# Order of index copies and exponentials on ScalarE in the first graph aggregation of a two-layer GNN and mixture-of-experts kernel

## The chip, the cores and the metric

The kernel runs on one core of one Trainium2 chip. The metric is the device time of one execution in microseconds, the median of several runs. The profile is of one execution on the same core.

## The reference

Four layers act on x, 3125 nodes by 256 features: an attention aggregation over a graph of 53125 edges, a mixture of eight experts, a weighted aggregation over the same graph with a batch norm, and a graph-routed mixture of four experts. The change lies in the first, which is, cut to what is computed:

```python
h = x @ Wn.T + bn                       # x layer-normed, 3125 x 256
e = edge_attr @ We.T + be
a = leaky_relu(sum((h[src] + e) * attn, axis=-1), 0.01)
m = segment_max(a, dst, num_segments=N)
a = exp(a - m[dst])
denom = segment_sum(a, dst, num_segments=N)
a = a / (denom[dst] + 1e-16)
out = relu(segment_sum(h[src] * a[..., None], dst, num_segments=N))
x = x + out
```

## The kernel before, in words

The edges are sorted by destination. They lie in chunks of 128 edges, one edge to a partition, and the destinations in 25 tiles of 128 nodes (`NT`). `emit_aggregate` (called twice, the first time with `softmax` true and the tag `a0`, the second time with the tag `a1`) sums, for every destination tile, over blocks of `BG` = 6 chunks. Most tiles have three blocks, some four, and there are 77 blocks, so 462 chunks with those that lie across a tile's edge counted twice. For the chunk at place `i` of block `g`:

- ScalarE copies the column of 128 source numbers into `idx[:, i]` (L574) and counts `indexed`.
- GpSimd (POOL) waits for that count and issues an indirect DMA, which gathers 128 rows of `h`, with a one behind each, from the table in HBM into `rows[:, i]` (L589).
- VectorE (DVE) writes for a whole block at once a mask `nb`: minus the tile's maximum where edge and destination belong together, and minus 1e30 besides where they don't (L722 and L726), into a ring of `RING` = 4 blocks. It counts `masked`.
- ScalarE makes the weights `w[:, i]` as the exponential of mask plus score (L789) and counts `weighed`.
- TensorE (PE) waits for the gather and for the weights and adds `w` transposed times `rows` to the tile's sum in PSUM (L619, two passes for float32), then counts `agg_done`, which frees `rows`, `idx` and `w` at place `i` alike.

The tiles' maxima are made ahead. During tile t VectorE masks the blocks of t (`mask_blocks`), adds the finished sum of t - 1 to x (`finish_tile`, L734 to L740) and then scans tile t + 2 (`scan`): for each of its blocks six masks (L684) and six maxima (L701), then one reduction (L704). PE transposes the result (L602, `find_max`), VectorE reduces it (L708, `negate_max`) and PE spreads it over the partitions (L606, `spread_max`); `keep_max` copies it into `negm` (L716), which is the first thing that VectorE does in a tile. PE's own order in tile t is: `find_max(t + 1)`, opening the sum (L612), the first block, `spread_max(t + 1)`, the other blocks, closing the sum (L623).

ScalarE's order is written out by hand. In every block there were six copies, each with its own wait for the freed place, then one wait for the mask, then six exponentials:

```python
put_indices(act, g, c)
act.wait_ge(masked, g + 1)
for i in range(BG):
    act.wait_ge(agg_done, g * BG + i + 1)
    nc.scalar.activation(w[:, i, :], ...)
```

where `put_indices` is

```python
for i in range(BG):
    act.wait_ge(agg_done, g * BG + i + 1)
    nc.scalar.copy(idx[:, i:i + 1], source[:, bass.ds(c + i, 1)]).then_inc(indexed, 1)
```

The blocks are a hardware loop (L783) in a loop over tiles (L780), whose bounds each engine loads from SBUF at a tile's start (L488).

Of the kernel before, what the change touches and what calls it, by code (L numbers as in the profile page):

```python
# [502 lines left out]
def emit_aggregate(nc, S, tag, table, softmax):  # L503
# [6 lines left out]
    indexed, agg_done, masked, weighed = sem(tag + "_idx"), sem(tag + "_agg"), sem(tag + "_msk"), sem(tag + "_w")  # L510
    best, best_t, negs, negs_w, closed, evac = (sem(f"{tag}_{n}") for n in ("best", "bestT", "negs", "negsW", "closed", "evac"))
    width = D + 1 if softmax else D
    with ExitStack() as ctx:
        sb = lambda n, s, d: ctx.enter_context(nc.sbuf_tensor(tag + n, s, d))
        idx = sb("idx", [P, BG], I32)
# [17 lines left out]
        source = S.src if softmax else S.esource  # L533
# [37 lines left out]
        def put_indices(act, g, c):  # L571
# [4 lines that stand above are left out]
        @block.gpsimd  # L576
        def _(pool):
            if softmax:
                total = tile_range(nc, pool, S, NT - 1)[0]
            else:  # L580
                total = pool.value_load(S.eranges[0:1, NT:NT + 1], min_val=1, max_val=EBLOCKS)
            count = pool.alloc_register(tag + "_count")
            pool.reg_mov(count, 0)
            with pool.Fori(0, total) as g:
                for i in range(BG):
                    pool.reg_add(count, count, 1)
                    pool.wait_ge(indexed, 1)
                    pool.wait_ge(indexed, count)
                    pool.indirect_dma_start(rows[:, i, 0:TW], None, table,  # L589
                                            bass.IndirectOffsetOnAxis(ap=idx[:, i:i + 1], axis=0)).then_inc(gathered[i], 16)  # L590
# [184 lines left out]
        @block.scalar  # L775
        def _(act):
            nc.scalar.preload_act_table(ACT.Exp)
            act.sem_inc(weighed, (RING - 1) * BG + 1)
            tiles = Tiles(act, "act")
            with act.Fori(0, NT) as t:  # L780
                tiles.load(t)
                tiles.step()
                with tiles.blocks() as g:  # L783
                    c = tiles.chunk(g)
                    put_indices(act, g, c)
                    act.wait_ge(masked, g + 1)
                    for i in range(BG):
                        act.wait_ge(agg_done, g * BG + i + 1)
                        nc.scalar.activation(w[:, i, :], nb[:, bass.ds(g % RING, 1), i, :].rearrange("p a n -> p (a n)"), ACT.Exp, bias=S.score[:, bass.ds(c + i, 1)]).then_inc(weighed, 1)  # L789


# [1049 lines left out]
```

## Time and profile before

| | us |
|---|---|
| median of 3 runs (lowest, highest) | 3857.48 (3857.24, 3864.25) |
| the profiled execution | 3854.0 |
| its span, first to last instruction | 3851.9 |
| first aggregation in it | 704 to 1515 |
| busy in the whole span: PE, DVE, ACT, POOL | 2660.5, 1510.2, 759.3, 1889.8 |

A time of the profile counts from the first instruction. An engine's idle time before an instruction is given with what ended it; "issue" means that nothing which the profile shows was waited for. PEld is TensorE's weight load, DVEq and ACTq are the instructions that a sequencer works off itself (registers, branches, waits); the page does not count these as busy.

### The profile page before, as it was taken

How to read it: one execution, taken by the hardware profiler on the slowest of the kernel's cores; microseconds unless marked ns; L12 is line 12 of the kernel's file. 1: busy time of each engine (PE TensorE's matmuls, PEld its weight loads, DVE VectorE, ACT ScalarE, POOL GpSimd, SP SyncE). 2: the span in 40 equal slices, each digit the busy share in tenths (PEclk: the TensorE clock that was granted, in tenths of full speed). 3: DMA queues.
4: the chain of work that ended last, by engine and by line, in shares of the span. 5: the costliest groups of instructions: out<-in, count | busy, mean ns of one | idle time of the engine just before them, and what ended most of it. 6: DMA issues, size and time to landing. Idle time of an engine off the chain costs nothing. (4 is left out here: it accounts for less than half of the span.)

```text
span 3851.9 us, 46754 instructions
## 1 busy us (share of the span) xinstructions
PE 2660.5 (69%) x10550; PEld 1816.4 (47%) x10551; DVE 1510.2 (39%) x3666; ACT 759.3 (20%) x2605; POOL 1889.8 (49%) x1926
## 2 busy tenths in 40 slices
PE   3249688465566556699999997677777755989900
PEld 2225587233333333576767665333333334666600
DVE  5774555656666653322222223322222233000075
ACT  0136000123322222222222221111111112222200
POOL 0000666265656554366666663366666611666602
PEclk9555555566666665799999998666666665999955
DMA  2012344132222222100000000233333311110001
GB/s 73 27 38 66 143 146 147 33 83 75 79 79 79 74 76 61 33 11 12 12 12 12 14 1 20 77 91 91 91 89 92 89 26 34 20 20 8 9 36 36
DMA packets 124782, 213.24 MB, mean 55 GB/s; under 512 B 56098, under 2 KB 82807, under 8 KB 122423
## 3 DMA queue, kind: packets, MB, share of 16 engines
q0 software_dynamic: 75808, 125.28, 13.1%
q1 hardware_dynamic: 48918, 87.37, 6.7%
q8 instruction: 18, 0.29, 0.0%
q14 instruction: 38, 0.30, 0.0%
HBM read 196.99 MB, written 15.52 MB: 55 GB/s over the span
## 5 line engine op out<-in xcount | busy, mean ns | idle before, releaser
L589 POOL DMA_INDIRECT a0rows<-table,a0idx x462 | 466.3, 1009 | 363.0 <-ACT a0idx L574 250.5
L589 POOL DMA_INDIRECT a1rows<-table,a1idx x444 | 420.1, 946 | 315.3 <-ACT a1idx L574 176.6
L619 PE MATMUL a1ps<-a1rows,a1w 128*128 128x256 f32 x888 | 435.5, 616 | 173.2 <-DMA a1rows<-table,a1idx 115.9
L619 PE MATMUL a0ps<-a0rows,a0w 128*128 128x257 f32 x924 | 428.3, 602 | 153.6 <-ACT a0w L789 71.4
L1053 POOL DMA_INDIRECT erecords<-k_rece x416 | 404.5, 972 | 213.3 <-issue 103.2
L881 PE MATMUL f0up<-k_xnT,f0w 128*128 x1280 | 386.0, 457 | 59.4 <-ACT f0hid L913 33.7
L1053 POOL DMA_INDIRECT records<-k_recg x288 | 301.0, 1045 | 226.1 <-POOLq L959 74.2
L1373 POOL DMA_INDIRECT gt_land<-table_gat,gt_source x281 | 265.9, 946 | 287.7 <-DVEq L1402 141.7
L619 PEld LDWEIGHTS a1ps<-a1rows,a1w 128*128 128x128 f32 x888 | 215.5, 284 | 393.2 <-issue 278.2
L619 PEld LDWEIGHTS a0ps<-a0rows,a0w 128*128 128x128 f32 x924 | 233.5, 286 | 345.8 <-issue 176.6
L891 PE MATMUL f0dn<-f0w,f0hid 128*128 128x256 f32 x1600 | 357.6, 380 | 9.2 <-issue 8.6
L881 PEld LDWEIGHTS f0up<-k_xnT,f0w 128*128 128x128 f32 x1280 | 246.5, 199 | 193.3 <-issue 57.7
L891 PEld LDWEIGHTS f0dn<-f0w,f0hid 128*128 128x128 f32 x1600 | 304.1, 190 | 56.2 <-issue 14.6
L832 DVE SCALAR_TENSOR_TENSOR k_x<-f0dn,k_gate,k_x 128x256 f32 (+1 forms) x200 | 88.9, 479 | 507.5 <-PE f0dn L891 330.1
L913 ACT ACTIVATE f0hid<-f0up,f0b1now 128x384 f32<-128x384 f32 (+1 forms) x320 | 167.7, 528 | 539.8 <-PE f0up L881 327.8
L658 DVE TENSOR_SCALAR a1w<-k_iota,k_elane,k_eweight 128x128 f32<-128x128 f32 x444 | 148.1, 370 | 266.1 <-PE a1ps L619 149.5
L1610 PE MATMUL f1dn<-gt_arena 128*128 128x256 f32 x800 | 191.0, 388 | 28.6 <-issue 24.3
L1600 PE MATMUL f1up<-k_xnT,gt_arena 128*128 x640 | 187.5, 449 | 23.5 <-DVE gt_arena L1417 14.1
L574 ACT COPY a1idx<-k_esource 128x1 int32 x444 | 82.7, 191 | 578.5 <-PE a1ps L619 351.8
L789 ACT ACTIVATE a0w<-a0nb,k_score 128x128 f32 x462 | 143.7, 389 | 235.1 <-DVE a0nb L726 183.0
L471 PEld LDWEIGHTS es_ps<-k_we_attn,es_ea 128*128 128x128 f32 x832 | 182.1, 332 | 5.6 <-issue 5.3
L1610 PEld LDWEIGHTS f1dn<-gt_arena 128*128 128x128 f32 x800 | 152.8, 193 | 62.1 <-issue 42.3
(387 smaller groups left out, 3133.3 us busy)
## 6 DMA issues: line engine op xcount, KB each, us to landing
es_ea<-in_eaT SPq DMA_DIRECT2D x16, 1664.0 KB
es_lane<-lane_row SPq DMA_DIRECT2D x16, 832.0 KB
so_rowl<-glane_row SPq DMA_DIRECT2D x32, 256.0 KB
a0rows<-table,a0idx POOLq DMA_INDIRECT x462
a1rows<-table,a1idx POOLq DMA_INDIRECT x444
erecords<-k_rece POOLq DMA_INDIRECT x416
table<-k_tbl SPq DMA_DIRECT2D x10, 650.0 KB, 3.6
records<-k_recg POOLq DMA_INDIRECT x288
```

Source lines behind the costliest of these rows:

```text
L471: nc.tensor.matmul(ps[i][:, 2, c:c + 1], ea[:, i, c * P:(c + 1) * P], S.we_attn[:, 0:1], start=True, stop=True).then_inc(step, 1)
L589: pool.indirect_dma_start(rows[:, i, 0:TW], None, table, bass.IndirectOffsetOnAxis(ap=idx[:, i:i + 1], axis=0)).then_inc(gathered[i], 16)
L619: nc.tensor.matmul(sum_of(t), w[:, i, :], rows[:, i, 0:width], start=False, stop=False).then_inc(agg_done, 1)
L658: nc.vector.tensor_scalar(w[:, i, :], S.iota[:, 0:P], S.elane[:, bass.ds(c + i, 1)], S.eweight[:, bass.ds(c + i, 1)], ALU.is_equal, ALU.mu ...
L789: nc.scalar.activation(w[:, i, :], nb[:, bass.ds(g % RING, 1), i, :].rearrange("p a n -> p (a n)"), ACT.Exp, bias=S.score[:, bass.ds(c + i ...
L881: ins = nc.tensor.matmul(up[q % 2][:, 0:size], w1[:, k, m * P:(m + 1) * P], S.xnT[:, k, bass.ds(g * (U * P) + a * P, size)], start=(k == 0 ...
L891: ins = nc.tensor.matmul(down[j][:, 0:D], hid[half][:, k, (j - a) * P:(j - a + 1) * P], w2[:, k, :], start=(k == 0), stop=(k == KH - 1))
L913: nc.scalar.activation(hid[half][:, m, :], up[q % 2][:, 0:(b - a) * P], ACT.Gelu, bias=bias_now[:, m:m + 1]).then_inc(hid_ready, 1)
L1053: pool.indirect_dma_start(self.rec_dram, bass.IndirectOffsetOnAxis(ap=self.rec[:, c + 1, 0:1], axis=0), self.rec[:, c + 1, 1:R], None).the ...
L1373: pool.indirect_dma_start(land[:, j, :], None, S.table_gat, bass.IndirectOffsetOnAxis(ap=source[:, j:j + 1], axis=0)).then_inc(gathered[la ...
L1600: ins = nc.tensor.matmul(up[q % 2][:, 0:size], w1[:, k, m * P:(m + 1) * P], S.xnT[:, k, bass.ds(g * (U * P) + a * P, size)], start=(k == 0 ...
L1610: ins = nc.tensor.matmul(down[j][:, 0:D], hid[half][:, k, (j - a) * P:(j - a + 1) * P], w2[:, k, :], start=(k == 0), stop=(k == KH - 1))
```

## The change

ScalarE, in the first aggregation alone, no longer copies six indices ahead of the wait for the block's mask. It waits for the mask first, and then makes for every place `i` one copy and one exponential, behind one wait for the freed place. `put_indices` remains for the second aggregation. The two other engines' programs are as before.

```diff
@@ -782,10 +782,10 @@
                 tiles.step()
                 with tiles.blocks() as g:
                     c = tiles.chunk(g)
-                    put_indices(act, g, c)
                     act.wait_ge(masked, g + 1)
                     for i in range(BG):
                         act.wait_ge(agg_done, g * BG + i + 1)
+                        nc.scalar.copy(idx[:, i:i + 1], source[:, bass.ds(c + i, 1)]).then_inc(indexed, 1)
                         nc.scalar.activation(w[:, i, :], nb[:, bass.ds(g % RING, 1), i, :].rearrange("p a n -> p (a n)"), ACT.Exp, bias=S.score[:, bass.ds(c + i, 1)]).then_inc(weighed, 1)
```

On ScalarE (the engine ACT), inside the loop over blocks, before the change; `a0idx` is `idx`, `k_src` the source numbers, `a0w` the weights and `a0nb` the mask, and an ISA row is a register or wait instruction. Here are the last two copies and the first two exponentials of a block:

```order
L574 ISA
L574 COPY a0idx<-k_src 128x1
L573 REGISTER_ALU
L574 ISA
L574 COPY a0idx<-k_src 128x1
L786 REGISTER_ALU
L789 ISA
L789 ACTIVATE a0w<-a0nb,k_score 128x128
L789 ISA
L789 ACTIVATE a0w<-a0nb,k_score 128x128
```

A block's six copies stand ahead of the wait for its mask (L786) and its exponentials behind it.

The same place after the change, two of a block's six pairs:

```order
L787 REGISTER_ALU
L788 ISA
L788 COPY a0idx<-k_src 128x1
L789 ISA
L789 ACTIVATE a0w<-a0nb,k_score 128x128
L787 REGISTER_ALU
L788 ISA
L788 COPY a0idx<-k_src 128x1
L789 ISA
L789 ACTIVATE a0w<-a0nb,k_score 128x128
```

Every copy now stands behind the wait for the block's mask and right ahead of the exponential of the same place.

## Rows read from the trace of the kernel before

**Rows 1.** Groups by line, 700 to 1515 us (busy us, mean ns, idle before them).

```profile
L619 PE MATMUL a0ps<-a0rows,a0w 128*128 128x257 f32 x924 | 428.3, 602 | 153.6 <-ACT a0w L789 71.4 <-DMA a0rows<-table,a0idx 59.8 <-issue 19.1
L789 ACT ACTIVATE a0w<-a0nb,k_score 128x128 f32 x462 | 143.7, 389 | 235.1 <-DVE a0nb L726 183.0 <-issue 46.0
...
L777 ACT ACT_TABLE_LOAD x1 | 1.3, 1283 | 310.9 <-PEq L306 310.9
```

**Rows 2.** Waits of 700 to 1515 us (total us, times, longest).

```profile
PEld a0psT L602 <- DVE a0top L704: 127.5, 18, 28.4
...
DVE a0rden L734 <- PE a0ps L623: 34.1, 2, 18.8
```

**Rows 3.** Line 716, a tile's first DVE instruction: ns, first and last start.

```profile
L716 DVE COPY a0negm<-a0psM x25: 280/292/293, 732.4 to 1471.6; 128x128 f32<-128x128 f32 x25
```

**Rows 4.** Timeline around the tile from 1108.76 us, part of it.

```profile
1108.76 0.29 DVE L716 COPY a0negm<-a0psM 128x128 f32<-128x128 f32 x1 [0.20 <-issue]
...
1112.04 1.86 ACT L789 ACTIVATE a0w<-a0nb,k_score 128x128 f32 x6 [8.99 <-DVE a0nb L726]
1112.17 0.29 DVE L708 TENSOR_REDUCE a0m<-a0psT 128x1 f32<-128x128 f32 x1 [0.34 <-issue]
...
1114.91 1.46 POOL L589 DMA_INDIRECT a0rows<-table,a0idx  x1 [4.65 <-ACT a0idx L574]
...
1122.37 1.26 DVE L684 TENSOR_SCALAR a0mb<-k_iota,k_dstf 128x128 f32 x6 [0.51 <-issue]
...
1126.41 0.75 DVE L684 TENSOR_SCALAR a0mb<-k_iota,k_dstf 128x128 f32 x2 [0.73 <-issue]
...
1129.65 0.94 POOL L589 DMA_INDIRECT a0rows<-table,a0idx  x1 [0.30 <-issue]
...
1132.53 0.70 PE L619 MATMUL a0ps<-a0rows,a0w 128*128 128x257 f32 x2 [0.42 <-DMA a0rows<-table,a0idx]
...
1133.05 1.08 ACT L574 COPY a0idx<-k_src 128x1 int32 x6 [4.47 <-PE a0ps L619]
...
1134.01 1.01 POOL L589 DMA_INDIRECT a0rows<-table,a0idx  x1 [3.41 <-ACT a0idx L574]
1135.16 1.26 DVE L684 TENSOR_SCALAR a0mb<-k_iota,k_dstf 128x128 f32 x6 [0.70 <-issue]
...
1139.50 0.29 DVE L716 COPY a0negm<-a0psM 128x128 f32<-128x128 f32 x1 [0.20 <-issue]
```

**Rows 5.** Sequencer instructions of line 684 and line 780, 1126 to 1132.5 us.

```profile
L684 DVEq FUSED_REGOPS  x6: 15/700/712, 1127.5 to 1132.4; - x6
...
L780 ACTq COMPARE_BRANCH  x1: 700/700/700, 1130.3 to 1130.3; - x1
```

**Rows 6.** Timeline of the four-block tile from 794.5 us: DVE, ACT, POOL.

```profile
815.32 0.51 DVE L684 TENSOR_SCALAR a0mb<-k_iota,k_dstf 128x128 f32 x2 [0.73 <-issue]
...
827.96 1.27 DVE L684 TENSOR_SCALAR a0mb<-k_iota,k_dstf 128x128 f32 x6 [0.70 <-issue]
...
817.69 0.19 ACT L574 COPY a0idx<-k_src 128x1 int32 x1 [1.94 <-issue]
...
823.58 0.94 POOL L589 DMA_INDIRECT a0rows<-table,a0idx  x1 [1.69 <-ACT a0idx L574]
```

**Rows 7.** DVE's timeline of the tiles from 1327.8 and from 1365.2 us.

```profile
1348.42 0.68 DVE L684 TENSOR_SCALAR a0mb<-k_iota,k_dstf 128x128 f32 x3 [0.73 <-issue]
...
1360.81 1.27 DVE L684 TENSOR_SCALAR a0mb<-k_iota,k_dstf 128x128 f32 x6 [0.98 <-issue]
...
1379.18 0.48 DVE L684 TENSOR_SCALAR a0mb<-k_iota,k_dstf 128x128 f32 x2 [0.95 <-issue]
...
1387.99 1.35 DVE L684 TENSOR_SCALAR a0mb<-k_iota,k_dstf 128x128 f32 x6 [0.73 <-issue]
```

**Rows 8.** Timeline of the last two tiles: first products of the earlier one, last close.

```profile
1461.29 5.36 PE L619 MATMUL a0ps<-a0rows,a0w 128*128 128x257 f32 x12 [0.95 <-ACT a0w L789]
...
1512.05 1.22 PE L623 MATMUL a0ps<-k_iota,k_zeros 1*128 1x257 f32 x2
```

## The prediction

> **What bounds the kernel now.** The change touches the first aggregation alone, 704 to 1515 us, so I read that stretch: first the groups by line, for how busy each engine is and what ended its idle time, then the waits, then the timeline of one tile for the order of events. PE's products take 428.3 of some 811 us and ScalarE's exponentials 143.7 [rows 1]; neither is full. ScalarE's idle time ahead of the exponentials is 235.1 us, of it 183.0 on VectorE's mask [rows 1]. PE waits 127.5 us, 18 times, for VectorE's scan [rows 2]. VectorE on the other side waits for PE at the sums 34.1 us in all, but only twice, with 18.8 the longest, where the work runs out [rows 2]. So **VectorE paces the tiles**: its first instruction of a tile starts 25 times, from 732.4 to 1471.6 us [rows 3], 30.8 us apart on average, and in the tile that I show from 1108.76 to 1139.50, 30.7 us [rows 4].
>
> Within that tile the reader is to see two things. First, ScalarE's exponentials wait 8.99 us for the mask and start at +3.3 us (1112.04), while the six copies for the same block had been made as soon as the places were free; those of the next tile stand at 1133.05, ten microseconds ahead of its mask [rows 4]. Copies, gathers and their latency lie under VectorE's scan. Second, the scan has **a dragging spell**. One block of it, from masks to masks, takes 4.04 us (1122.37 to 1126.41), the next one 8.75 us (1126.41 to 1135.16) [rows 4]. In the spell the register instructions ahead of the masks take 700 ns in the median, and so does ScalarE's branch at the tile's end [rows 5]. The spell begins at 1127.5 [rows 5], 12.6 us after the first of 12 gathers that POOL issues back to back (1114.91 to 1129.65) [rows 4], and ends at 1132.4, 2.8 us after the last one was issued, when its rows reach PE (1132.53) [rows 4, 5]. I don't know its mechanism; I use what it goes with, an unbroken run of about ten gathers and the landing of the last. In a four-block tile ScalarE is still copying for its fourth block when the spell comes, one copy in 2.1 us, and POOL, still issuing, breaks off only for 1.69 us ahead of 823.58; there the same block of the scan takes 12.64 us (815.32 to 827.96) [rows 6].
>
> **The change, part by part.** Nothing is added in busy time: 462 copies and 462 exponentials stay. There is one table load in the stretch, though copies and exponentials alternated in sixes [rows 1], so alternating singly should load none.
>
> (a) *Exponentials ahead of time.* A block's first exponential no longer stands behind the sixth copy, so PE's gap at a block's start goes: at most 0.95 us, as at 1461.29 [rows 8]. In the tiles that VectorE paces this is worth nothing, because PE ends its tile at about +24.4 us (its last pair starts at 1132.53 and takes 0.7) and then waits [rows 4].
>
> (b) *Copies behind the mask.* What was queued behind the copies on POOL and PE moves with them. At a tile's start the first copy now comes at +3.3 instead of before the tile. From copy to gather is 0.96 us (1133.05 to 1134.01), so POOL begins at +4.3. A tile of three blocks has 18 gathers; at 0.94 + 0.30 us each the last starts 21.1 us on, at +25.4 [rows 4]. The gather beside a mask takes 1.46 instead of 0.94 us [rows 4]; before, about two of them met masks, now perhaps two to four, and I add 0.9: +26.3. From the last gather to its product are 2.9 us (1129.65 to 1132.53), 0.6 for the pair: +29.8, with the close and the transpose of the next maximum about +31 [rows 4]. VectorE wants that maximum at 3.4 us of the next tile (1112.17) [rows 4], at +34.1 with the period of before. So the later gathers are hidden, with 3 us to spare.
>
> The Trainium skill ("SBUF — State Buffer", section "Who interferes with whom") says that VectorE and GpSimd share a port pair and that the one that comes second is blocked for the other's whole instruction. By that, four instructions of 0.96 us would hold the gathers 3.8 instead of 0.9 us, and with the pause below the maximum would come 0.3 us too late in each of 22 tiles, 3921 instead of 3914 us. The row of 1.46 us shows a hold of half an instruction, and I go by it.
>
> (c) *One long run of gathers in place of two.* Before, POOL had six gathers and twelve by turns, with idle time of 3.41 us ahead of the six (1134.01) and 4.65 us ahead of the twelve (1114.91) [rows 4]. Now all 18 follow each other from +4.3. If the spell still sets in 12.6 us behind a run's start, it comes at +17, ahead of the third block's copies, not behind all of them (+18.7 before). ScalarE then has to make some five copies in the spell, each with four sequencer instructions to the pair where there were three, and POOL goes on until it starves; the spell ends only when the rows have landed. That is the state of the four-block tile. VectorE is then held as there. I have three tiles in which gathers and copies overlap a spell like this: 12.64 us [rows 6], 12.39 us (1348.42 to 1360.81) and 8.81 us (1379.18 to 1387.99) [rows 7], against 8.75 in an ordinary tile. The excess is 3.9, 3.6 and 0.1, on average 2.5 us. **22 tiles x 2.5 = 56 us**, bounds 2 and 86 us. A starved pause of 3 us moves PE's end to +34, and VectorE's wish to 33.2 + 3.4 = +36.6, so the chain stays hidden.
>
> (d) *The last two tiles*, where no scan is left and PE and the gathers decide: 36 places from 1461.29 to 1512.05, 1.41 us each [rows 8]. The first product comes 3.4 us later (0.96 + 2.9 - 0.45), and up to five gaps of at most 0.95 us go, 0 to 4.7, of which I take half: **+1 us**, bounds -1.3 and +3.4. The first tile's delay is under VectorE's work.
>
> Sum: 56 + 1 = +57 on the profiled execution's 3854.0, which is 3.5 us under the median; on the median of 3857.5 that is **3914 us**.
>
> **The rivals.**
>
> *The spell goes away, and the kernel is faster.* If the spell comes from ScalarE's burst of six exponentials beside VectorE's masks, and not from the gathers, single exponentials dissolve it. For it: ScalarE's own instructions behind a burst are slow in the same spell [rows 5]. Against it: the burst at 1112.04 brings none, and the spell lasts until the rows land [rows 4, 5]. VectorE would win 8.75 - 4.04 = 4.7 us a tile, but then the maximum at +31 decides (c. 27.6 us a tile): 3.1 x 22 = 68, so about 3790 us; a spell only shortened lies between.
>
> *Nothing changes within 0.2%.* ScalarE's own drag starves POOL at once, the run is cut after ten to twelve gathers, and the spell costs VectorE as much as before. The tile of 8.81 us speaks for it. 3857.5 + 1 = about 3859 us.
>
> *The gather chain takes over, slower still.* If the third block is held up by two pauses of 3 us and each mask holds a gather fully (+2.9), the maximum comes at 31 + 6 + 2.9 = +39.9, the period is 36.5 and the time 3857.5 + 22 x 5.8 = about 3985 us. It decides from a lag of 5.6 us over (b) on. Against it: one starved pause should let the rows land and end the spell.
>
> **How the numbers follow.** The forecast (3860 to 3944 by its bounds) has 0.60, the vanished or shortened spell 0.19, no change 0.13, the gather chain 0.08. A difference of 0.2%, 7.7 us, is about what a measurement of this kernel can tell from none. Of the forecast's 0.60 some 0.02 fall within that: slower 0.66, same 0.15, faster 0.19. The range is 3830 to 3955: it holds the forecast, no change, a third of the faster case and a quarter of the chain's, together 0.81.
>
> **What would show it.** Right: in the changed profile the first copy of a tile follows the mask by a few tenths; POOL's gathers of a tile form one run from +4.3 us; a block of the scan with 700 ns register instructions takes over 10 us in most tiles; the tile's period is 32.5 to 34 us; PE's wait for the scan (L602) shrinks from 127.5 us while VectorE still waits for nobody. Wrong: a period under 30 us and no such instructions (the burst was the cause), or a period unchanged with the spell as long as before, or VectorE waiting at L708 for PE's transpose (the chain took over).

## The result, and the profile after

The changed kernel takes 3910.78 us (median of 4 runs, 3904.23 to 3916.50), the kernel before beside it 3860.86 (3857.24 to 3866.64): ratio 1.0127, 95% interval 1.0105 to 1.0149, **50 us slower**. The forecast was 3914. Every execution counted here and below is of the usual, fast kind.

The profiled execution after took 3916.5 us, the highest of the four, so the two traces lie 62.5 us apart and the medians 50. The page's first rows, the costliest groups by line of 700 to 1570 us (busy us, mean ns, idle before them), PE's wait for VectorE's scan and VectorE's first instruction of a tile, all of the changed kernel:

```profile
span 3914.4 us, 46677 instructions
PE 2725.5 (70%) x10550; PEld 1790.9 (46%) x10551; DVE 1502.1 (38%) x3666; ACT 748.6 (19%) x2605; POOL 1873.9 (48%) x1926
```

```profile
L619 PE MATMUL a0ps<-a0rows,a0w 128*128 128x257 f32 x923 | 506.6, 649 | 249.3 <-DMA a0rows<-table,a0idx 222.8 <-issue 8.7 <-ACT a0w L789 7.2
...
L789 ACT ACTIVATE a0w<-a0nb,k_score 128x128 f32 x462 | 182.1, 400 | 0.0
L701 DVE SCALAR_TENSOR_TENSOR a0top<-a0mb,k_score,a0top 128x128 f32<-128x128 f32 x462 | 141.1, 349 | 156.1 <-issue 140.7
...
L788 ACT COPY a0idx<-k_src 128x1 int32 x462 | 85.0, 184 | 640.1 <-DVE a0nb L726 288.2 <-PE a0ps L619 208.4 <-issue 143.4
```

```profile
PEld a0psT L602 <- DVE a0top L704: 53.2, 10, 28.4
...
L716 DVE COPY a0negm<-a0psM x25: 280/292/293, 731.7 to 1526.5; 128x128 f32<-128x128 f32 x25
```

Against [rows 1] PE's wait for weights falls from 71.4 to 7.2 us, so the exponentials are indeed out of its way, and in its place stands a wait for gathers, 222.8 us where it was 59.8. ScalarE's copies, which waited for PE alone, now wait 288.2 us for the mask besides. PE's wait for VectorE's scan falls from 127.5 us [rows 2] to 53.2: PE has less time left in a tile. Against [rows 3] the 24 tiles between the first and the last start take 794.8 instead of 739.2 us.

Where VectorE loses the time is seen in its idle time inside the scan, ahead of the masks (L684) and the maxima (L701). The kernel before had there, in 700 to 1515 us:

```profile
L701 DVE SCALAR_TENSOR_TENSOR a0top<-a0mb,k_score,a0top 128x128 f32<-128x128 f32 x462 | 136.6, 348 | 68.5 <-issue 52.5
L684 DVE TENSOR_SCALAR a0mb<-k_iota,k_dstf 128x128 f32 (+1 forms) x462 | 109.0, 304 | 106.4 <-issue 106.4
```

and the changed kernel, besides the row of L701 above:

```profile
L684 DVE TENSOR_SCALAR a0mb<-k_iota,k_dstf 128x128 f32 (+1 forms) x462 | 101.3, 297 | 69.3 <-issue 69.3
```

That is 174.9 us of idle time before and 225.4 after, **+50.5**, while the busy time of the two lines falls by 3.2. Most of it is put down to "issue": VectorE waits for no other engine, it stands behind its own sequencer, as in the dragging spell of the kernel before.

Two tile starts and the last close tell when the time came in. First the kernel before, then the changed one; the close of before is in [rows 8], at 1512.05.

```profile
1431.42 0.29 DVE L716 COPY a0negm<-a0psM 128x128 f32<-128x128 f32 x1 [0.20 <-issue]
```

```profile
1481.18 0.29 DVE L716 COPY a0negm<-a0psM 128x128 f32<-128x128 f32 x1 [0.20 <-issue]
...
1570.99 1.22 PE L623 MATMUL a0ps<-k_iota,k_zeros 1*128 1x257 f32 x2
```

These are the starts of the 23rd tile. The first 22 tiles take 749.5 instead of 699.0 us, **+50.5**, the last three, to the close, 89.8 instead of 80.6, **+9.2**; with a start 0.7 us earlier the last close comes 58.9 us later, of the 62.5 us between the two spans.

One tile of the changed kernel, in order of time (compare [rows 4]):

```profile
1137.31 0.29 DVE L716 COPY a0negm<-a0psM 128x128 f32<-128x128 f32 x1 [0.20 <-issue]
...
1138.39 0.47 PE L602 MATMUL a0psT<-k_ident,a0top 128*128 128x128 f32 x1
...
1140.70 0.19 ACT L788 COPY a0idx<-k_src 128x1 int32 x1 [11.36 <-DVE a0nb L726]
1140.71 0.29 DVE L708 TENSOR_REDUCE a0m<-a0psT 128x1 f32<-128x128 f32 x1 [0.34 <-issue]
...
1141.68 0.94 POOL L589 DMA_INDIRECT a0rows<-table,a0idx  x1 [7.60 <-ACT a0idx L788]
...
1144.63 7.70 PE L619 MATMUL a0ps<-a0rows,a0w 128*128 128x257 f32 x12 [4.61 <-DMA a0rows<-table,a0idx]
...
1150.91 1.07 DVE L684 TENSOR_SCALAR a0mb<-k_iota,k_dstf 128x128 f32 x5 [0.51 <-issue]
...
1154.47 0.35 DVE L701 SCALAR_TENSOR_TENSOR a0top<-a0mb,k_score,a0top 128x128 f32<-128x128 f32 x1 [1.86 <-issue]
...
1156.90 0.94 POOL L589 DMA_INDIRECT a0rows<-table,a0idx  x1 [0.30 <-issue]
...
1161.13 0.94 POOL L589 DMA_INDIRECT a0rows<-table,a0idx  x1 [3.29 <-ACT a0idx L788]
...
1161.68 1.34 DVE L684 TENSOR_SCALAR a0mb<-k_iota,k_dstf 128x128 f32 x6 [0.73 <-issue]
...
1165.77 1.42 DVE L684 TENSOR_SCALAR a0mb<-k_iota,k_dstf 128x128 f32 x6 [0.70 <-issue]
...
1170.27 0.29 DVE L716 COPY a0negm<-a0psM 128x128 f32<-128x128 f32 x1 [0.20 <-issue]
```

The tile takes 33.0 us. The first copy follows the mask at +3.4, the first gather starts at +4.4, and 13 gathers follow each other without a break until 1157.8; then POOL starves for 3.29 us and issues the other five. The scan's first block takes 10.77 us (1150.91 to 1161.68), the next 4.09. So it is in nearly every scan: by VectorE's timelines the held block takes 9.7 to 12.0 us in 23 scans of the changed kernel, over 10 in all but one, and in the kernel before 8.1 to 9.1 us in 21 scans, 12.6 and 12.4 in two. PE's transpose (1138.39) is done before VectorE reads it, which is why L708 waits for nothing: VectorE still paces. The spell is seen in the sequencer's instructions ahead of the maxima, min/median/max ns, 732 to 1481 us, changed kernel:

```profile
L701 DVEq ALU_OP  x414: 4/40/727, 744.5 to 1479.4; - x138
```

### The profile page after: what moved, and what is told of

Same layout as the page of the kernel before. It is cut to its first block and busy times, and to the rows that moved or that the text cites. A ratio compares the mean times of both kernels' runs of the same rounds, so it can differ in the third digit from the quotient of the medians.

```text
span 3914.4 us, 46677 instructions
## 1 busy us (share of the span) xinstructions
PE 2725.5 (70%) x10550; PEld 1790.9 (46%) x10551; DVE 1502.1 (38%) x3666; ACT 748.6 (19%) x2605; POOL 1873.9 (48%) x1926
## 5 line engine op out<-in xcount | busy, mean ns | idle before, releaser
L619 PE MATMUL a0ps<-a0rows,a0w 128*128 128x257 f32 x924 | 507.1, 649 | 249.3 <-DMA a0rows<-table,a0idx 222.8
L589 POOL DMA_INDIRECT a0rows<-table,a0idx x462 | 449.8, 974 | 438.6 <-ACT a0idx L788 292.7
L619 PE MATMUL a1ps<-a1rows,a1w 128*128 128x256 f32 x888 | 421.9, 598 | 188.9 <-DMA a1rows<-table,a1idx 131.5
L619 PEld LDWEIGHTS a0ps<-a0rows,a0w 128*128 128x128 f32 x924 | 212.5, 286 | 531.4 <-issue 427.2
L788 ACT COPY a0idx<-k_src 128x1 int32 x462 | 85.0, 184 | 640.1 <-DVE a0nb L726 288.2
L701 DVE SCALAR_TENSOR_TENSOR a0top<-a0mb,k_score,a0top 128x128 f32<-128x128 f32 x462 | 141.1, 349 | 156.1 <-issue 140.7
L574 ACT COPY a1idx<-k_esource 128x1 int32 x444 | 82.7, 191 | 582.6 <-PE a1ps L619 363.0
```

The costliest lines, as they stand in the source:

```text
L589: pool.indirect_dma_start(rows[:, i, 0:TW], None, table, bass.IndirectOffsetOnAxis(ap=idx[:, i:i + 1], axis=0)).then_inc(gathered[i], 16)
L619: nc.tensor.matmul(sum_of(t), w[:, i, :], rows[:, i, 0:width], start=False, stop=False).then_inc(agg_done, 1)
L701: nc.vector.scalar_tensor_tensor(top[:, i % (BG // 2), :], mb[:, i, :], S.score[:, bass.ds(c + i, 1)], top[:, i % (BG // 2), :], ALU.add, ...
```

## The experiments

A thing first without which the numbers can't be read. Beside the first four experiments the kernel before took 3858 us, about as in the measurement of the change (3861). Beside all later ones it took 3507 to 3509 us, and there **the dragging spell does not occur**: none of those traces has, in its whole length, a register or branch instruction of VectorE or ScalarE near 700 ns, where the trace of the kernel before has some 250. The chip's number doesn't tell which comes, since chip 0 stands beside both. So each run is compared with the kernel before beside it, and the condition is named: *with the spell* or *without*.

### With the spell: which part of the change costs

**Copies behind the mask, but six and six.**

```diff
-                    put_indices(act, g, c)
                     act.wait_ge(masked, g + 1)
+                    put_indices(act, g, c)
```

> The order of before, six copies and then six exponentials, but with the wait for the block's mask moved ahead of the copies: the place of the copies relative to the mask changes, the alternation does not. Theory (moving a tile's first gathers behind its mask makes one long run of 18 gathers, and VectorE's scan is held by the dragging spell): as slow as the change, 3900 to 3920 us, tile period 32.5 to 34 us. Rival (the alternation itself costs, by four sequencer instructions to a pair instead of three): 3855 to 3868 us, period 30.7 us.

Measured: 3922.44 us, ratio 1.0184 (1.0148 to 1.0219). The whole loss is there without any alternation, and 14 us more than the change's 50, also just above the 3920 expected: the place of the copies is enough for it. Why sixes behind the mask cost more than pairs isn't shown.

**The first block of a tile as before, the others alternating.**

```diff
-                with tiles.blocks() as g:
+                with tiles.first_block() as g:
+                    c = tiles.chunk(g)
+                    put_indices(act, g, c)
+                    act.wait_ge(masked, g + 1)
+                    for i in range(BG):
+                        act.wait_ge(agg_done, g * BG + i + 1)
+                        nc.scalar.activation(w[:, i, :], ...)
+                with tiles.other_blocks() as g:
...
```

(against the changed kernel; the second loop holds its pairs)

> A tile's first block keeps the order of before (six copies, the mask, six exponentials), the other blocks alternate as in the change: the alternation stays, the copies of a tile's first block are again hidden under the scan. Theory (the place of the first copies decides): POOL's gathers fall again into six and twelve, period 30 to 31 us, 3850 to 3868 us. Rival (the alternation itself costs): most of the loss stays, over 3885 us.

Measured: 3899.48 us, ratio 1.0121 (1.0088 to 1.0153). Of the two theories the number fits the rival's (over 3885): 41 us of the loss stayed although the first block's copies were ahead again. But the timeline of this kernel shows that the edit did not do what its theory asked for, to bring back the gathers' old places (a tile's start, and the first gather of its run of twelve):

```profile
1127.41 0.29 DVE L716 COPY a0negm<-a0psM 128x128 f32<-128x128 f32 x1 [0.20 <-issue]
...
1135.48 1.18 POOL L589 DMA_INDIRECT a0rows<-table,a0idx  x1 [5.50 <-ACT a0idx L795]
...
1149.52 0.95 POOL L589 DMA_INDIRECT a0rows<-table,a0idx  x1 [0.30 <-issue]
...
1153.71 1.03 POOL L589 DMA_INDIRECT a0rows<-table,a0idx  x1 [3.24 <-ACT a0idx L574]
...
1159.22 0.29 DVE L716 COPY a0negm<-a0psM 128x128 f32<-128x128 f32 x1 [0.20 <-issue]
```

The run starts at +8.1, where it was +6.2 [rows 4]: now the *second* block's copies wait for its mask, which comes 2 us after the places are free. I had thought of the first block alone. The run ends later in the scan, most held blocks take 9.2 to 10.1 us instead of 8.1 to 9.1, this tile takes 31.8 us, and some take 34.9. The alternation as such is not cleared by this run; that is left to a later one.

**Pauses on GpSimd, in the kernel before and in the change.** The same edit in both, an experiment on what brings the spell:

```diff
                                             bass.IndirectOffsetOnAxis(ap=idx[:, i:i + 1], axis=0)).then_inc(gathered[i], 16)
+                if softmax:
+                    pool.wait_ge(gathered[BG - 1], g * 16 + 16)
```

> The kernel before, with one wait more on GpSimd: in the first aggregation it waits after each block of six gathers until the last of them has landed. No run is longer than six. Theory (an unbroken run of about ten gathers brings the spell): register instructions of 700 ns are gone, a block of the scan takes 4.0 instead of 8.75 us, and the period falls from 30.7 to 26 to 29 us, where the chain of gathers and products takes over: 3790 to 3830 us. Rival (the spell comes from ScalarE's burst or from VectorE's own instructions): spell as before, 3857 us or more, up to 3900 by the gathers' delay.

> The change, with the same wait on GpSimd after each block of six gathers. Theory (the change loses by the spell in VectorE's scan): the spell is gone, VectorE no longer paces; the chain mask, three times six gathers with a landing each, transposed maximum, gives a period of 30 to 32 us, so 3840 to 3885 us, faster than the change although gathers wait more. Rival (the change loses because the gathers' latency stands bare behind the mask): every pause adds to it, 22 tiles by 3 to 5 us, 3960 to 4010 us.

Measured: 3883.80 us in the order of before (1.0061, 1.0041 to 1.0081) and 3889.99 in the order of the change (1.0088, 1.0055 to 1.0121). Both miss their ranges, 3790 to 3830 and 3840 to 3885. The sequencer's instructions ahead of the masks and VectorE's waits in the order of before, then the same in the change's order (lines are two higher than in the kernel before):

```profile
L686 DVEq FUSED_REGOPS  x452: 4/57/77, 706.6 to 1459.2; - x151
...
DVE a0m L710 <- PE a0psT L604: 132.2, 23, 13.0
```

```profile
L686 DVEq FUSED_REGOPS  x452: 17/57/77, 703.5 to 1465.8; - x151
...
DVE a0m L710 <- PE a0psT L604: 143.3, 24, 13.0
```

The longest such instruction takes 77 ns, where it was over 700: **with no run over six gathers the spell is gone** from the first aggregation, in both kernels (of VectorE's and ScalarE's other register and branch instructions there, three take 675 to 708 ns in the first kernel and none in the second). The second aggregation has no pauses, and there 48 and 65 such instructions of some 700 ns remain, where the kernel before has 57. What VectorE won it gave back waiting for PE's transpose, 132 and 143 us. A pause costs more than I had put: between the sixth gather and the next block's first lie 3.0 us idle,

```profile
1106.46 0.95 POOL L589 DMA_INDIRECT a0rows<-table,a0idx  x1 [2.94 <-ACT a0idx L574]
...
1116.93 0.94 POOL L589 DMA_INDIRECT a0rows<-table,a0idx  x1 [3.01 <-ACT a0idx L574]
```

so a block takes 10.47 us and a tile of three 31.4, not 26 to 29. This is why the first of the two missed its range by 54 us. The second misses by 5, with a period inside its 30 to 32 us, and the direction is its theory's: a delay added to every block of the change makes it *faster*, 3890 us (3882 to 3892) against 3911 (3904 to 3917), with 3858 and 3861 for the kernel before beside them. The rival, that the change loses by bare latency, asked for 3960 or more. With the spell out of both, 6 us lie between the two orders, instead of 50, and their executions overlap. The 6 don't tell what the late copies cost without a spell, because here the pauses pace both; the changed kernel without pauses, further down, tells that.

### Without the spell

**Copies and exponentials alternate only from a tile's third block on**, where the mask is made long before.

```diff
-                with tiles.blocks() as g:
+                with act.Fori(tiles.block, tiles.block + 2) as g:
...
+                with act.Fori(tiles.block + 2, tiles.stop) as g:
+                    c = tiles.chunk(g)
+                    act.wait_ge(masked, g + 1)
+                    for i in range(BG):
+                        act.wait_ge(agg_done, g * BG + i + 1)
+                        nc.scalar.copy(idx[:, i:i + 1], source[:, bass.ds(c + i, 1)]).then_inc(indexed, 1)
+                        nc.scalar.activation(w[:, i, :], ...)
```

(against the kernel before; the last tile, of two blocks, keeps one loop in the order of before)

> The first two blocks of a tile keep the order of before, the third and fourth (whose masks are made long before) alternate single copies and exponentials; so the alternation is there, but no copy comes later for its mask. Theory (what costs is that copies wait for masks, a tile's first block for a new tile's mask and the second for a mask 2 us after the place is free): 3850 to 3868 us, period 30.2 to 31 us. Rival (the alternation itself costs): over 3870 us.

Measured: 3507.49 against 3506.65 us, 1.0001 (0.9992 to 1.0011). The alternation costs nothing and brings nothing, where no copy comes later for it. The expected figures were for the other condition; the ratio is what they said. With the spell this kernel wasn't measured.

**The changed kernel again.**

> The changed kernel once more, since in the call before the kernel before took 3507 us, 351 us less, and in four traces there no register instruction took 700 ns. If that chip or one like it runs this: theory (without the spell VectorE needs 26.2 us a tile, and the change then loses because the chain mask, 18 gathers, products, transposed maximum takes about 28.5 us): 3540 to 3570 us against 3507. Rival (the spell was the whole of the loss): within 10 us of 3507. On a chip with the spell: 3900 to 3920 against 3858.

Measured: 3547.70 against 3508.06 us, 1.0121 (1.0104 to 1.0138): 40 us, with no spell at all. Of the kernel before there is no trace in this condition; the run just told stands for it, since its time is the same. Its tile starts and its gathers, then those of the changed kernel, with the instructions ahead of its masks and its wait for the transpose (660 to 1600 us):

```profile
L716 DVE COPY a0negm<-a0psM x25: 280/292/293, 684.7 to 1318.8; 128x128 f32<-128x128 f32 x25
...
L589 POOL DMA_INDIRECT a0rows<-table,a0idx x462 | 475.9, 1030 | 235.9 <-ACT a0idx L574 118.1 <-issue 112.9 <-ACT a0idx L795 4.9
```

```profile
L716 DVE COPY a0negm<-a0psM x25: 279/292/293, 684.7 to 1356.6; 128x128 f32<-128x128 f32 x25
...
L684 DVEq FUSED_REGOPS  x427: 52/57/77, 680.7 to 1332.5; - x143
...
DVE a0m L708 <- PE a0psT L602: 50.2, 18, 6.9
```

24 tiles take 634.1 us with the copies ahead, 26.4 each, and 671.9 with the change, 28.0 each: +37.8 of the 40. None of the instructions ahead of the masks is over 77 ns. Now VectorE does wait, 18 times and 50.2 us, for the transposed maximum; the waits are as in the tile from 1134.00 us, where the transpose comes at +3.8:

```profile
1134.00 0.29 DVE L716 COPY a0negm<-a0psM 128x128 f32<-128x128 f32 x1 [0.20 <-issue]
...
1137.79 0.47 PE L602 MATMUL a0psT<-k_ident,a0top 128*128 128x128 f32 x1
1138.30 0.29 DVE L708 TENSOR_REDUCE a0m<-a0psT 128x1 f32<-128x128 f32 x1 [1.23 <-PE a0psT L602]
```

So without the spell the chain mask, 18 gathers, products, transpose decides, which the prediction had put at 27.6 us a tile.

**Three ways of thinning out the gathers of the kernel before.** They were made to shorten or avoid the spell and ran in the condition without one; they tell the price of delayed gathers alone.

```diff
+                    if softmax and i:
+                        pool.wait_ge(gathered[i - 1], g * 16 + 16)
```

> The kernel before; in the first aggregation GpSimd, having issued the gather of place i (1 to 5), waits until that of place i - 1 has landed, so that hardly more than two are under way and about 1.45 us lie between gathers instead of 1.25. Theory A (the spell comes when gathers follow each other faster than something behind them works them off): spell gone or late, tile period 27 to 29.5 us, 3790 to 3835 us. Theory B (only a full pause, in which the last gather lands, keeps the spell away): 700 ns instructions still there, period 31 us or more, 3860 to 3890 us.

```diff
+                    act.wait_ge(gathered[BG - 1], g * 16)
                     put_indices(act, g, c)
```

(on ScalarE, in every block but a tile's first)

> The kernel before; ScalarE, ahead of the copies of every block but a tile's first, waits until the last gather of the block before has landed. The run of twelve in a tile's middle becomes six and six with a pause of some 3 us; between tiles nothing is added. Theory (runs of ten and more bring the spell): no spell in the scan's second block (4 us instead of 8.75), period 26.5 to 29 us by what runs of twelve arise across the tile's edge, 3770 to 3835 us. Rival (the pause only delays the gathers): 3857 us or more.

```diff
+                if softmax:
+                    pool.wait_ge(gathered[BG - 2], g * 16 + 16)
```

> As the run with a pause on GpSimd after every block, but the pause ends when the fifth of the six gathers has landed, 1.2 us earlier: a block of gathers takes about 9.2 instead of 10.4 us. Theory A (a short break is enough): hardly a 700 ns instruction, period 3 x 9.2 = 27.6 us, 3857 - 22 x 3 = 3790, at most 3830 us. Theory B (all rows must have landed): spells come back, period 29 us and more, 3840 to 3880 us.

Measured: 3705.91 us (1.0561, 1.0543 to 1.0578), 3576.44 (1.0197, 1.0180 to 1.0214) and 3536.19 (1.0082, 1.0065 to 1.0099). All delay the gathers and none has a spell to remove, so their theories on it stay untested. In the first VectorE waits 197.2 us for the transpose:

```profile
DVE a0m L710 <- PE a0psT L604: 197.2, 23, 17.1
```

Of the two last, the one with a pause shorter by a gather after every block costs 30 us, the one that holds ScalarE costs 70.

**The scan by blocks**, with three VectorE instructions in place of twelve, in the order of before and in that of the change:

```diff
-                    for i in range(BG):
-                        mask(mb, t, c, i)
+                    nc.vector.tensor_tensor(mb[:], S.iota[:, bass.ds(t * P, P)].unsqueeze(1).to_broadcast([P, BG, P]),
+                                            S.dstf[:, bass.ds(c, BG)].unsqueeze(2).to_broadcast([P, BG, P]), ALU.not_equal)
                     v.drain()
-                    for i in range(BG):
-                        if i == BG // 2:
-                            v.drain()
-                        nc.vector.scalar_tensor_tensor(top[:, i % (BG // 2), :], ...)
+                    nc.vector.scalar_tensor_tensor(mb[:], mb[:], -BIG, S.score[:, bass.ds(c, BG)].unsqueeze(2).to_broadcast([P, BG, P]),
+                                                   ALU.mult, ALU.add)
+                    v.drain()
+                    nc.vector.tensor_tensor(top[:], top[:], mb[:], ALU.max)
                     v.drain()
```

> The kernel before, with the scan of a block in three VectorE instructions of 128x768 (unequal, times -1e30 plus score, maximum) in place of twelve of 128x128, so with a quarter of the register instructions: undisturbed about 3.6 instead of 4.05 us a block. Theory (the spell holds VectorE by its register instructions): on a chip with the spell a block in it takes under 5.5 instead of 8.75 us, period 25 to 28 us, 3760 to 3810 us against 3858. Rival (the spell holds data instructions as well): period 29.5 us and more, over 3830. On a chip without it 3485 to 3507 us.

> The change with the same scan. Theory (what the change loses is the longer spell in the scan, then the chain of gathers): on a chip with the spell the period falls from 33.3 to 29 to 32 us, as VectorE no longer paces but ScalarE's held copies and the 18 gathers do: 3820 to 3890 us, slower than the same scan in the order of before by 40 to 100 us. Rival (the change costs VectorE nothing but the register instructions): equal within 15 us to the run before. On a chip without the spell 3530 to 3570 us, over 35 us slower than the run before.

> The scan by blocks in the order of before once more, since its first run met a chip on which nothing in the aggregation is held. If this run meets the spell (the kernel before at 3858 us): theory (the spell holds VectorE by its register instructions, of which this scan has a quarter): a tile period of 25 to 28 us, 3760 to 3810 us; rival (data instructions are held as well, or the held copies of ScalarE pace the tiles): period 29.5 us or more, over 3830 us. If not (3508 us): 3499 to 3508 us as before, which tells the theories not apart.

Measured: 3504.59 us (0.9988, 0.9978 to 0.9997) and, the same kernel again, 3507.25 (0.9992, 0.9983 to 1.0002); in the change's order 3547.63 (1.0115, 1.0099 to 1.0132). Neither run of the first was in the condition with the spell, so whether it holds register instructions alone stays open. In the change's order the gain of some 3 us is gone too: 43 us slower than the same scan in the order of before, as its theory had it for this condition. The new scan in the order of before is 0.1% faster than the kernel before in its first measurement, and the second does not tell it from nothing.

## Why the prediction was right

The mechanism was right where it decides: the late copies make a spell that holds a block of VectorE's scan longer, and VectorE still paces. The size was right in part by luck, in (c) and in the sum.

**What bounds, and (a) exponentials ahead of time: right.** VectorE paced the tiles before and after, and PE's gap at a block's start was worth nothing. The wait for weights went from 71.4 to 7.2 us without any gain, and alternation alone measures 1.0001, in the condition without the spell.

**(b) Copies behind the mask: right in place, a little off in size.** First gather at +4.3 forecast, +4.4 measured; transpose of the maximum at +31 forecast, +34 with a starved pause, and about +34 measured (1138.39 is 1.1 us into the next tile, and a tile takes 33). VectorE wants it at +36.4 and did not wait. What masks and gathers cost each other I had read too coarsely. First a mask of the kernel before, beside which stands the gather of 1114.91 [rows 4], then a mask and a gather of the changed kernel:

```profile
1114.59 0.96 DVE L726 SCALAR_TENSOR_TENSOR a0nb<-a0ne,a0negm 128x768 f32 x1 [0.34 <-issue]
```

```profile
1144.78 0.96 DVE L722 TENSOR_TENSOR a0ne<-k_iota,k_dstf 128x768 f32 x1 [0.69 <-issue]
1145.43 1.13 POOL L589 DMA_INDIRECT a0rows<-table,a0idx  x1 [0.30 <-issue]
```

At 1114.91 the mask had 0.64 us to go and the gather took 0.51 us longer than 0.95; at 1145.43 it was 0.31 and 0.18. So it is nearly throughout both traces: a gather that starts inside a mask is longer by what is left of the mask, less 0.13 us. A mask that starts inside a gather takes its 0.96 us as ever (183 times), and so does the gather. Hence the hold hangs on who comes first, and it fell where I had put 0.9 us a tile more: all 462 gathers took 466.3 us before and take 449.8 after, the two rows being

```profile
L589 POOL DMA_INDIRECT a0rows<-table,a0idx x462 | 466.3, 1009 | 363.0 <-ACT a0idx L574 250.5 <-issue 112.5
```

```profile
L589 POOL DMA_INDIRECT a0rows<-table,a0idx x462 | 449.8, 974 | 438.6 <-ACT a0idx L788 292.7 <-issue 145.9
```

The Trainium skill ("SBUF — State Buffer", "Who interferes with whom") counts a VectorE instruction with two inputs in SBUF against a GpSimd instruction that reads SBUF among the cases in which whichever comes second is fully blocked. The traces agree for a gather that comes second, and not for a mask that does. The prediction's sum by that rule, 3921 us, gave every mask a gather that waits for its whole length, which no gather did.

**(c) One long run of gathers: the step that carries the result. The effect was right, the run less so, the size in part luck.** The held block takes 10.8 instead of 8.75 us in the tile shown, "over 10" was forecast; the period there is 33.0, forecast 32.5 to 34; the 22 tiles lose 50.5 us, 2.3 each, forecast 56.

The 18 gathers do not make one run: 13, a break of 3.29 us, then five, where it was 12 and 6. So the long run is hardly longer. What grew is the part of it that was still to come when the spell set in. In the kernel before, the spell of the tile in [rows 4] sets in after ten of twelve gathers and lasts 4.9 us. In the tile of 1137.31 the first register instruction of 700 ns starts at 1151.6, 9.9 us after the run's start and after eight of 13 gathers, and the last such ends at 1160.0, 3.1 us after the start of the run's last gather (1156.90): 8.5 us. In most tiles of the kernel before two or three gathers were still to come at the onset, in the changed kernel about five. Forecast was 12.6 us from the run's start; so the spell met the scan's first block, not its second. Why it comes earlier isn't shown.

The 2.5 us a tile were the average of three tiles of the kernel before with 3.9, 3.6 and 0.1. The changed kernel has neither kind: the held block is 2 to 3 us longer in nearly every tile. That the average of two extremes came out near the usual tile was luck. The two four-block tiles among the 22 lose nothing, 37.4 us for 37.8 and 36.3 for 37.4, and the tiles behind them 4.7 and 4.3.

One premise was wrong without consequence: ScalarE has three sequencer instructions for a copy and its exponential in either order, as the listings of the change show, and not four where there were three.

The cause is tested with the spell: copies behind the mask suffice for the whole loss, and where runs are cut to six, the spell goes and the change gets faster.

**(d) The last tiles: mis-sized.** The term was +1 us, bounds -1.3 and +3.4, for the last two tiles. From the 23rd tile's start to the close it measured +9.2 us, in two parts. The scan of the 23rd tile was still running and held as the others: that tile takes 29.3 instead of 26.3 us, start to start, which I had not counted. The last two tiles themselves, from the 24th's start to the close, take 6.1 us more, beyond my upper bound. Their first products, before (the 24th tile's is in [rows 8]) and after:

```profile
1495.02 7.46 PE L619 MATMUL a0ps<-a0rows,a0w 128*128 128x257 f32 x12 [1.06 <-DMA a0rows<-table,a0idx]
```

```profile
1517.64 2.52 PE L619 MATMUL a0ps<-a0rows,a0w 128*128 128x257 f32 x4 [0.66 <-DMA a0rows<-table,a0idx]
...
1553.45 8.74 PE L619 MATMUL a0ps<-a0rows,a0w 128*128 128x257 f32 x14 [1.42 <-DMA a0rows<-table,a0idx]
```

The first comes 3.5 us later in its tile, as forecast (3.4). From it to the last tile's first are 35.8 instead of 33.7 us, and from there to the close 17.5 instead of 17.0. So no gap was won: PE there waits for gathers, not for weights. What the 2.1 us are was not taken apart; one thing that differs is PE's granted clock, 0.50 of full speed in these two tiles, the lower of its levels, where it was 0.59, and a pair of products takes 1.22 us, hardly less than the 1.25 from gather to gather, where many took 0.70.

In the sum, on the profiled executions, +57 was forecast and the first aggregation lost 58.9 us, because the 8 us too few in (d) and the 5.5 too many in (c) nearly cancel: luck again.

**The rivals.** The faster one held that a vanished spell leaves 3790 us. The spell did vanish, from both kernels, in the second condition; the cost of the changed order did not, 40 instead of 50 us. Its own bound, the maximum at c. 27.6 us a tile, is what then decides (28.0 measured). "Nothing changes" did not happen in either condition. "The gather chain takes over" did, but only where there is no spell, and at 1.6 us a tile instead of 5.8.

**What stays open.** What the spell is, and why it is absent in one condition: there the gathers follow each other more densely (idle time before them 235.9 us where it was 363.0, and mostly 18 in a run where it was 6 and 12), so a long run is needed for it, as the pauses show, but is not enough. Whether it holds only register instructions was not tried with the spell present. The kernel before is some 350 us faster without it, and the 24 tiles account for 105 of them (739.2 against 634.1). Other stages with indirect gathers are faster there too: the 281 of the last mixture lie within 353 us instead of 411, though the trace of the kernel before has no slow register instructions beside them. So the two conditions differ in more than the spell, and the 40 us without it can't be taken off the 50 with it.

## What to carry to other kernels

When a transfer's index, descriptor or address is made on an engine that also makes the operand which goes with it, issue the first ahead of the wait that belongs only to the second: a copy of 0.19 us put behind a mask moved the gathers, with 2.9 us from the last one to its product, later against everything else, and cost 50 and 40 us where the PE gaps that the neater order removed were worth nothing. Before a gap on one engine is worth closing, find which engine paces the loop. And where a stretch of the old trace already shows the new overlap, as three tiles did here, the price can be read from there, but look how far the samples lie apart before trusting their average.

## What the runs showed of the hardware

- After mostly 8 to 11 indirect gathers of 128 rows in unbroken sequence, 1.25 us apart, register and branch instructions of ScalarE and VectorE took 700 ns instead of some 50, until the last gather's rows had landed. It occurred in all traces of one condition, in the two with pauses only outside the stage that had them, and in no trace of the other condition, where the same kernel took 3507 instead of 3858 us.
- A gather that started inside a VectorE instruction of 128x768 with two inputs in SBUF took longer by what was left of that instruction, less 0.13 us (1.46 instead of 0.95 us with 0.64 left). The VectorE instruction that started inside a gather was never longer than 0.96 us.
- Waiting on GpSimd for a landing after six gathers left it idle 3.0 us; waiting inside a block for the gather before made the kernel 199 us slower, where I had expected 0.2 us a gather, which is an estimated 92 us for all 462.
- A loss of the same size, 50 and 40 us, came from two different bounds in the two conditions: VectorE's held scan in the one, VectorE's wait for PE's transpose in the other.
